# Second attention of a gated two-layer block: TensorE's order within a unit as a written list, with ten scores items of a later unit instead of five

## The reference

```python
def _L1_xattn_ref(x, mem, Wq, Wkv, Wout, bout):      # HEADS = 16, d = 16, mem_len = 64
    q = x @ Wq
    k, v = jnp.split(jnp.concatenate((mem, x), axis=1) @ Wkv, 2, axis=-1)
    ...                                               # to heads: (4, 16, 1024 or 1088, 16)
    dots = jnp.einsum('bhid,bhjd->bhij', q, k) * scale
    dots = jnp.where((j_idx > i_idx + mem_len)[None, None], -jnp.inf, dots)
    attn = jax.nn.softmax(dots, axis=-1)
    out = jnp.einsum('bhij,bhjd->bhid', attn, v)
    return out.transpose(0, 2, 1, 3).reshape(b, n, dim) @ Wout + bout
```

## Time and profile before

| | |
|---|---|
| median of 3 runs | 1718.27 us (1717.44 to 1722.09) |
| the profiled execution | 1718.15 us, span 1716.5 us |
| TensorE busy in the span | 1154.1 us, 67% |
| VectorE busy in the span | 1075.8 us, 63% |
| granted TensorE clock, mean | 0.825 of full speed |

### The profile page before, as it was taken

How to read it: one execution, slowest core, us unless ns; L and a number is a source line. 1 busy time by engine, 2 the same in 40 slices (tenths; PEclk the granted TensorE clock), 3 DMA queues, 4 the chain that set the end, 5 groups by cost and what they waited for, 6 DMA issues and landing times. The chain is left out here.

```text
span 1716.5 us, 28020 instructions
## 1 busy us (share of the span) xinstructions
PE 1154.1 (67%) x8147; PEld 584.4 (34%) x8159; DVE 1075.8 (63%) x2419; ACT 619.7 (36%) x893; POOL 524.6 (31%) x607
## 2 busy tenths in 40 slices
PE   3799963422427777676076837878878788888776
PEld 2455541211214444443033412323323233332455
DVE  4989865432414444444587547878868778885475
ACT  0455532111101111121022303556655566656530
POOL 1333325557525555555211051111111111111110
PEclk7999986555658888887578856989989999999998
DMA  5011001112277556652476541121111111110002
GB/s 184 19 37 37 19 10 71 68 62 100 97 202 165 129 134 145 138 141 40 177 236 219 149 129 34 35 55 47 34 35 35 54 49 34 34 35 2 1 0 98
DMA packets 190212, 141.19 MB, mean 82 GB/s; under 512 B 127368, under 2 KB 162955, under 8 KB 190106
## 3 DMA queue, kind: packets, MB, share of 16 engines
q1 hardware_dynamic: 164906, 81.49, 18.9%
q0 software_dynamic: 18848, 50.70, 8.2%
q10 hardware_dynamic: 6352, 7.54, 1.3%
HBM read 53.56 MB, written 69.01 MB: 71 GB/s over the span
## 5 line engine op out<-in xcount | busy, mean ns | idle before, releaser
L1726 DVE TENSOR_REDUCE small<-ps 128x1 f32<-128x480 f32 (+6 forms) x768 | 419.0, 595 | 103.3 <-PE ps L1778 95.8
L1704 ACT ACTIVATE region<-ps 128x1024 f32<-128x1024 f32 (+5 forms) x384 | 322.8, 880 | 234.7 <-PE ps L1835 233.2
L1676 POOL TENSOR_SCALAR_AFFINE_SELECT region<-region 128x512 f32<-128x512 f32 (+2 forms) x160 | 87.3, 546 | 495.8 <-ACT region L1704 495.8
L867 POOL DMA_INDIRECT token_rows<-region,small x174 | 171.2, 984 | 164.9 <-DVE small L1082 117.9
L1851 PE MATMUL ps<-region 128*32 128x512 f32 (+5 forms) x1792 | 201.3, 510 | 29.6 <-POOL region L1676 21.1
L1778 PE MATMUL ps<-region 48*128 48x480 f16 (+6 forms) x896 | 158.3, 342 | 46.3 <-DVE small L1726 45.8
L1207 PE MATMUL ps<-region 128*128 128x384 f16 x696 | 151.1, 378 | 33.2 <-DMA region<-expert_rows 33.1
L1218 PE MATMUL ps<-region 128*128 x522 | 83.2, 316 | 88.0 <-DVE region L1097 86.4
L859 POOL DMA_INDIRECT expert_rows<-region,small x128 | 125.5, 980 | 54.9 <-issue 37.5
L1835 PE MATMUL ps<-region 50*128 50x512 f16 (+5 forms) x896 | 132.8, 332 | 12.2 <-issue 10.0
L1773 PE MATMUL ps<-small 64*128 64x128 bf16 (+1 forms) x768 | 91.4, 249 | 38.0 <-DMA region<-v_parts 18.7
(11 more groups left out here) (243 smaller groups left out, 1760.5 us busy)
## 6 DMA issues: line engine op xcount, KB each, us to landing
region<-token_rows POOLq DMA_DIRECT2D x16, 1024.0 KB, 8.0
v_parts<-region SPq DMA_DIRECT2D x16, 576.0 KB, 5.8
region<-v_parts SPq DMA_DIRECT2D x16, 576.0 KB, 4.1
region<-k_parts SPq DMA_DIRECT2D x96, 68.0 KB, 2.2
region<-q_parts SPq DMA_DIRECT2D x96, 64.0 KB, 2.2
k_parts<-region SPq DMA_DIRECT2D x16, 272.0 KB, 3.6
x_sb<-in_x ACTq DMA_DIRECT2D x8, 512.0 KB, 9.0
region<-in_w13T SPq DMA_DIRECT2D x16, 256.0 KB, 2.9
```

What stands on the lines that cost most here:

```text
L867: nc.gpsimd.indirect_dma_start(out=ys, out_offset=bass.IndirectOffsetOnAxis(ap=home[:, g % HOMES, j:j + 1], axis=0), in_=y_out[:, b, j, :] ...
L1676: nc.gpsimd.affine_select(out=t, in_=t, compare_op=ALU.is_ge, fill=0.0, base=r0, pattern=[[0, G], [1, w]], channel_multiplier=-1).then_inc ...
L1704: nc.scalar.activation(dst, src, ACT.Exp, scale=SCALE).then_inc(s_exp, 1)
L1726: nc.vector.tensor_reduce(nmp[:, qt, half, p0:p0 + np_, place], bank[:, 0:np_ * nk].rearrange("p (h k) -> p h k", h=np_), AX.X, ALU.max).t ...
```

## The change

The computed list is replaced by one that is written out, `AHEAD` becomes 10, and `first_plan` makes ten N items instead of five. The order of T and PV items among themselves stays, except that `Tn` 0 and 1 come behind N4, and no engine has an instruction more or less over the whole run. What one unit holds stays too: 24 S and N items, of which 14 and 10 where 19 and 5 were. `plan_14` then holds 14 S items where it held 19, and `first_plan` holds 34 S and N items where it held 29.

```diff
-        S_SHARE, MT_SHARE = 0.80, 0.85
-        AHEAD = 5
...
-        main = []
-        for k in range(len(steps)):
-            main += [("T", i) for i, (kk, _) in enumerate(t_list) if kk == k and k]
...
-            while now and put_now < keys_now * done / (total * S_SHARE):
...
-        plan += closing
+        AHEAD = 10
+        ORDER = """T2 PV0 T3 S10 PV1 T4 T5 S11 PV2 T6 S12 T7 S13 PV3 T8 S14 T9 PV4 S15 T10 S16 PV5 S17 T11 PV6
+                   oT0 T12 S18 T13 PV7 T14 S19 T15 S20 PV8 T16 S21 T17 PV9 S22 T18 T19 S23 PV10 T20 T21 PV11
+                   mT0 N0 T22 T23 PV12 N1 N2 N3 PV13 N4 Tn0 Tn1 N5 N6 N7 oT1 N8 N9"""
...
+        plan = [item(word) for word in ORDER.split()]
...
-        first_plan = [("S", i) for i in range(len(s_list))] + [("mT", 0)] + [("S2", i) for i in range(AHEAD)] + closing[:FIRST_T]
+        first_plan = [("S", i) for i in range(len(s_list))] + [("mT", 0)] + [("S2", i) for i in range(AHEAD)] + closing
```

More of the change, by code:

```diff
@@ L1565, in flamingo, with item @@
-        assert not now and not later
-        plan += closing
+        AHEAD = 10
+        ORDER = """T2 PV0 T3 S10 PV1 T4 T5 S11 PV2 T6 S12 T7 S13 PV3 T8 S14 T9 PV4 S15 T10 S16 PV5 S17 T11 PV6
+                   oT0 T12 S18 T13 PV7 T14 S19 T15 S20 PV8 T16 S21 T17 PV9 S22 T18 T19 S23 PV10 T20 T21 PV11
+                   mT0 N0 T22 T23 PV12 N1 N2 N3 PV13 N4 Tn0 Tn1 N5 N6 N7 oT1 N8 N9"""
+        def item(word):
+            kind = word.rstrip("0123456789")
+            return {"N": "S2"}.get(kind, kind), int(word[len(kind):])
@@ L1567, in flamingo @@
+        plan = [item(word) for word in ORDER.split()]
+        assert [i for kind, i in plan if kind == "S"] == list(range(AHEAD, len(s_list)))
+        assert [i for kind, i in plan if kind == "S2"] == list(range(AHEAD))
+        assert [i for kind, i in plan if kind == "T"] == list(range(FIRST_T, len(t_list)))
+        assert [i for kind, i in plan if kind == "PV"] == list(range(len(steps)))
+        closing = [("Tn", i) for i in range(FIRST_T)]
         plan_14 = [p for p in plan if p[0] != "S2"]
```

## The result

The changed kernel is slower: 1738.44 us median against 1720.24 in 20 runs each, a ratio of 1.010 with a 95% interval of 1.0078 to 1.0122. That is 17 to 18 us, where 13 were forecast (1731 us), within the range. Two executions in the slower state of the chip, 1751.40 us here and 1931.72 us in experiment 7 (mean clock 0.616), stand outside the ratios.

A forecast was written before the change was run, and what follows sets the result against it. It took TensorE and VectorE, neither full, to bound the steady unit by waiting for each other in turn. Terms -4 + 7.0 - 1.5 + 11.5 gave +13 on 1718.15: 1731 us, range 1705 to 1747.

The forecast's parts named there:

- The clock: End of each unit, PV13 to PV0: 16.5 falls to 1.2 GHz against 5, +11.5 us (bounds 0 and +22).
- The steady unit at full clock: Units that follow `plan`: 32.7 us against 33.04, so -4 us over 14 units.
- The list: Hand walk through the new unit noting where VectorE stands idle: 4.3 us in sum against 4.66 before.
- `first_plan`: Ahead of unit 0: N5 to N9 added, wholly on the path, +7.0 us.
- Unit 14: Five S items fewer, with TensorE and ScalarE setting its length: -1.5 us (bounds -0.5 and -3).
- The jumps: Three stretches holding TensorE's loop jump: same matmuls, clock falls either way, 0, at most +1.5 us each.
- the two ends: Ahead of unit 0, five more N items, +7.0 us; in unit 14, five fewer S items, -1.5 us.
- the case of 1720 us: Rival: at unit ends the clock falls no more often than now; +1.5 us, no change; chance 0.16.
- The faster case: Rival: 1.5 us of VectorE's waits for TensorE goes in each unit, -21 us, 1703 us; chance 0.21.
- the much slower case: Rival: two clock falls in every unit, longer jumps, unit 0.5 us longer than walked: 1753 us; chance 0.13.

The follow-up runs named there:

- experiment 7: Kernel before with four idle matmuls a unit and those ahead of unit 0: 1679.91 us, 0.9891; another chip 1701.44, 0.9863; changed kernel with both sets 1712.39, 0.9909.
- experiment 2: Changed kernel with four idle matmuls a unit, two ahead of N6 and two ahead of N9: 1721.29 us in its only run.
- experiment 3: Kernel before with four idle matmuls a unit, one ahead of N4 and three ahead of S5: 1709.83 us, 0.9933 of the kernel before.
- experiment 6: Kernel before with 30 idle matmuls ahead of the first scores item and two behind each scores item ahead of unit 0: 1708.71 us, 0.990.
- experiment 1: Changed kernel with eight idle matmuls a unit in TensorE's waits from N5 to N9: 1714.71 us, 0.9953 of the kernel before.

## Why the prediction was right, and where its terms were off

Its direction, its main mechanism and its size held. That the size came so close is partly luck, since errors of single terms, up to 5 us, fell on both sides. By its own steps:

**The clock** was the largest term, +11.5 us, and measured +14.7 (experiments 2 and 3; 12 with the seven falls of experiment 6). The place was right: the stretch from PV13 to PV0, with six scores items in it. The term was small because half of the falls were taken as short and half as long. All eleven were long, the mean clock of a unit being 0.90 where the single falls of before left 0.95. The price was right: 21.1 / 11 = 1.9 us for a long fall, just under 1.0 for each half of it, where 1.0 was taken.

**The steady unit at full clock** was -4 us over 14 units and is about +1; over the eleven units without a jump +0.4 is measured. The largest listed waits of VectorE were nearly right one by one: 1.52 at mT0 against 1.55, 0.67 before N1 against 0.6, and 0.42 before S10 in experiment 1 (its timeline below) against 0.6. The step that failed is the comparison. The list held only the gaps worth naming, 4.3 us, and was set against 4.66, which is the whole of a unit's length less VectorE's busy time and holds the short ones too, such as those between the reciprocal and the product. Measured the same way the new unit has 33.12 - 28.33 = 4.79. Of this the profile names 3.0 + 1.5 = 4.5 us as waits, near the list, and 0.3 are short gaps. Before it names 3.0 + 0.7 = 3.7, and 1.0 are short gaps. So the named waits grew by 0.8 and the short gaps shrank by 0.7, which no list of single waits shows.

```profile
1450.83 0.26 DVE L1730 RECIPROCAL small<-ps 128x16 f32<-128x16 f32 x1
1451.23 0.42 DVE L1732 TENSOR_TENSOR region<-ps,small 128x256 f32 x1
1451.58 2.47 DVE L1710 TENSOR_REDUCE small<-ps 128x1 f32<-128x512 f32 x4
1454.47 2.13 DVE L1710 TENSOR_REDUCE small<-ps 128x2 f32<-128x384 f32 x4 [0.42 <-PE ps L1762]
```

**`first_plan`** was +7.0 and is +6.8: the same shapes in the same stage made the best kind of estimate. **Unit 14** was -1.5 and is -2.4. **The start of unit 0** wasn't in the sum: its first half holds two scores items fewer and took 16.3 us instead of 18.9, -2.6. The stages ahead, which nothing touched, differed by 2.3 us between the two traces. **The jumps** were 0 and measured +4.8; but the same three stretches sum to 114.1 to 125.5 us over the kernels here, whatever their order, so this difference isn't shown to be the order's. The standstill of TensorE at the jump was 3.3, 3.4 and 3.3 us before and 3.6, 4.7 and 4.7 after, which is 3 of the 4.8 us; over all kernels it was 3.0 to 4.7. Why it varies stays open.

Against the forecast the terms moved by +4.4 (unit: -4 to +0.4), +3.2 (clock), -3.7 (the two ends with the start of unit 0), +4.8 (jumps) and -1.2 (stages that nothing touched): 13 became the 20.5 us between the two traces, where the medians of the 20 runs each differ by 18.2.

**The rivals.** The clock does fall more often; the case of 1720 us fails, and with it the rule it rested on, that only long stops of TensorE matter: between PV13 and PV0 no wait is over 1.08 us in any of the eleven units. The faster case fails on the unit, 33.13 us at full clock. Of the much slower case the long fall in every unit came true; it was put at +22 us and measured +14.7. Part of each fall lies over N8 and N9, which VectorE paces: its reductions of them took 2.67 us against 2.47 at full clock (experiment 1), while the wait ahead of S10 grew from 0.42 to 1.86. The Trainium skill's rule on short idle moments among PSUM banks ("TensorE: Matmul & The Clock Gate", section "A second HAM failure mode: psum-queue depth-cycling") agrees with these traces, where the clock fell at the ends of eleven units without a wait over 1.08 us.

## What to carry to other kernels

Before moving work that another engine paces (here six scores items at VectorE's 1.1 us each) into one stretch, look at what TensorE then does in that stretch: where it was thin here, the clock fell, and the dense work behind it paid. A few idle matmuls on constants, put into waits that exist anyway, show in one run how much of a time is the clock's, and can stay in as a gain (0.986 to 0.989 here, with those ahead of unit 0). When gaps of an engine are listed by hand, don't set the named ones against the whole of its idle time: the short gaps change with the order as well. And don't expect a gap that is closed to be won: here the next item inherited it.

## What the runs showed that was not expected

- Four idle matmuls of 512 columns a unit kept the clock at 1.00 in eleven of eleven units, where without them it fell in each (new order, experiment 2) or in five (old order, experiment 3, where TensorE's busy time in a unit went from 27.79 to 28.55 us).
- A stage that VectorE paces, busy 31.8 and 31.7 us, took 39.2 us at 1.2 GHz and 34.0 at 2.4 (experiment 6). At 1.2 GHz VectorE idled 0.18 to 0.27 us ahead of the items of the earlier trace rows.
- The three units that hold a jump of TensorE's loop took 37.2 to 43.6 us each over all kernels, with idle matmuls at the end of the unit or without, and with a fall of the clock each time. Why one such unit takes 6 us more than another wasn't settled.
